# Transposing by DMA instead of on TensorE in a two-layer graph attention kernel

## The reference

```python
def layer0(x, adj):                 # one head, softmax over the query axis
    alpha = relu((x @ wq0) @ (x @ wk0).T) * (adj != 0)
    return softmax(alpha, axis=1) @ (x @ w0)

def layer1(y, adj):                 # 16 heads of 32
    q, k, v = heads(y @ Wq + bq), heads(y @ Wk + bk), heads(y @ Wv + bv)
    s = where(adj == 0, -inf, q @ k.T / sqrt(32))
    return merge(softmax(s, axis=-1) @ v) @ Wo + bo

y   = layernorm(x + layer0(x, adj))
out = layernorm(y + layer1(y, adj))
```

## Time and profile before

| | us |
|---|---|
| median of 3 runs (lowest and highest) | 2967.58 (2967.09 to 2967.93) |
| the profiled execution, span from first to last instruction | 2967.6 |
| one pass, from one group's load to the next | 89.65 |
| TensorE busy in the span | 2902.2 |
| VectorE busy | 2365.3 |
| ScalarE busy | 2016.6 |
| GpSimd busy | 582.6 |
| share of the 16 DMA engines taken by the SP queue's packets | 23.3% |

### The profile page before, as it was taken

How to read it: one execution, slowest core, us unless ns; L and a number is a source line. 1 busy time by engine, 2 the same in 40 slices (tenths; PEclk the granted TensorE clock), 3 DMA queues, 4 the chain that set the end, 5 groups by cost and what they waited for, 6 DMA issues and landing times. The chain is left out here.

```text
span 2967.6 us, 65967 instructions
## 1 busy us (share of the span) xinstructions
PE 2902.2 (98%) x24264; PEld 1775.5 (60%) x24264; DVE 2365.3 (80%) x4627; ACT 2016.6 (68%) x6414; POOL 582.6 (20%) x1289
## 2 busy tenths in 40 slices
PE   7899999999999999999999999999999999999996
PEld 4565666656666656666666666666666666666554
DVE  4588888888888788888788888888888888888886
ACT  3476676666676766676767766767776766776665
POOL 1121122121122121121121221121221211221210
PEclk9999999999999999999999999999999999999997
DMA  3222122222122222122221122221122221222220
GB/s 121 61 72 76 43 56 73 57 76 72 37 65 61 69 76 62 40 72 54 76 76 54 48 72 54 76 76 47 51 76 54 76 76 42 57 71 59 75 53 24
DMA packets 96369, 188.06 MB, mean 63 GB/s; under 512 B 18608, under 2 KB 34992, under 8 KB 96048
## 3 DMA queue, kind: packets, MB, share of 16 engines
q1 hardware_dynamic: 96048, 183.84, 23.3%
HBM read 49.55 MB, written 33.55 MB: 28 GB/s over the span
## 5 line engine op out<-in xcount | busy, mean ns | idle before, releaser
L647 ACT ACTIVATE e<-sm,nmax 128x128 f32<-128x128 f32 x2048 | 791.1, 391 | 27.6 <-DVE nmax L776 25.6
L598 ACT ACTIVATE qk<-front,bqk 128x512 f16<-128x512 f32 x256 | 175.9, 687 | 381.6 <-PE front L429 381.6
L825 POOL TENSOR_TENSOR ln<-ln 128x1 f32<-128x1 f32 x256 | 49.0, 192 | 1890.2 <-DVE ln L804 1496.6
L647 ACT ACTIVATION_READ_ACCUMULATOR e<-sm,nmax 128x1 f32 x2048 | 391.0, 191 | 0.0
L664 DVE SCALAR_TENSOR_TENSOR pT<-pt_bank,pT 128x512 f16<-128x512 f32 x512 | 348.9, 681 | 42.6 <-ACT pT L653 42.1
L653 ACT ACTIVATE pT<-pt_bank 128x512 f16<-128x512 f32 x512 | 302.8, 591 | 103.6 <-PE pt_bank L543 101.6
L776 DVE TENSOR_REDUCE nmax<-sm 128x4 f32<-128x512 f32 x512 | 351.3, 686 | 17.7
L429 PE MATMUL fin_bank<-W_O,oT 128*128 128x512 f16 x1536 | 356.3, 382 | 1.4 <-DVE oT L664 1.4
L429 PE MATMUL front<-W_V,yT 128*128 128x512 f16 x1536 | 354.0, 380 | 0.0
L429 PE MATMUL front<-xT,W_A 128*128 128x512 f16 x1536 | 353.6, 380 | 0.3 <-DVE xT L664 0.3
L429 PE MATMUL front<-yT,W_Q 128*128 128x512 f16 x1536 | 352.2, 379 | 1.6 <-DVE yT L664 1.6
(11 more groups left out here) (111 smaller groups left out, 4482.3 us busy)
## 6 DMA issues: line engine op xcount, KB each, us to landing
q_st<-qk SPq DMA_DIRECT2D x384, 128.0 KB, 2.4
k_st<-qk SPq DMA_DIRECT2D x384, 128.0 KB, 2.4
x_sb<-in_x SPq DMA_DIRECT2D x128, 256.0 KB, 3.4
out_x<-z_sb SPq DMA_DIRECT2D x128, 256.0 KB, 2.5
adj_i<-in_adj SPq DMA_DIRECT2D x32, 256.0 KB, 4.6
y_sb<-in_L_gnn_wq SPq DMA_DIRECT2D x1, 1024.0 KB, 5.6
yb<-in_L_gnn_wk SPq DMA_DIRECT2D x1, 1024.0 KB, 8.1
x_p<-in_L_gnn_weight SPq DMA_DIRECT2D x1, 1024.0 KB, 10.5
```

Of the source, the lines that this page charges most:

```text
L598: i = act.activation(dst, src, ACT.Identity, bias=bias, scale=scale)
L647: act.activation(e1[:, k % 2, h, :], sm[:, k % SM_BUFS, h, :], ACT.Exp, bias=nmax[:, k % SM_BUFS, h:h + 1], accum_out=esum[:, n % 2, head: ...
L825: pool.tensor_tensor(ln[:, 8:9], ln[:, 7:8], ln[:, 8:9], ALU.add).then_inc(moments, 1)
```

## The change

The five kinds of transpose leave TensorE. Their inputs are first split into fp16 HI and LO parts in SBUF, side by side, and one DMA from the SP queue transposes both parts at once. For x: `x_parts` (HI on ScalarE, LO now on VectorE instead of GpSimd), then DMA `xT`. For y: `y_parts` (HI on ScalarE, LO on GpSimd), then DMA `yT`. For the probabilities: `P` (HI and LO from `e1` in SBUF instead of from PSUM), then DMA `pT`, from two buffers `p_p` into four buffers `pT`. For the attention output: `o_parts` (HI on ScalarE, LO on GpSimd), then DMA `oT`. For adj: DMA `adjT` of the fp16 tile `adj01`. Each of these DMAs moves 128 partitions of 1024 fp16 values (256 KB, eight blocks of 128x128), `adjT` 512 values (128 KB, four blocks). The `q` and `k` steps wait for all four `yT` DMAs of the group, `t` for all four `xT` DMAs.

The freed banks go to the front jobs (four banks instead of three) and to `S` (two instead of one). The stacking is cut into eight pieces of three DMAs that other steps can stand between. The order is a new list, `PASS`, with ages from -1 to 2, which also gives the first and the last passes (no order of its own for the drain). Two memsets of eps per normalisation go (the addition is fused on GpSimd), and the scale X_SCALE moves from the evictions to the parts and the normalisation.

The core of the diff:

```diff
-LATE = (2, 3)
-def pass_order(): ...
-def drain_order(): ...
+P_BUFS = 2
+PT_BUFS = 4
+PASS = [
+    ...
+    ("norm1", 2, 2), ("PV", 0, 1), ("norm0", 0, 0), ("y_parts", 0, 0), ("pT", 4, 1), ("oT", 0, 1),
+    ("g", 1, 0), ("S", 5, 1), ("pT", 5, 1), ("yT", 0, 0), ("residual1", 3, 1), ("fin", 3, 2), ("PV", 1, 1), ("o", 0, 1),
+    ("exp", 4, 1), ("P", 4, 1), ("exp", 5, 1), ("o_parts", 0, 1), ("norm0", 1, 0), ("g", 2, 0), ("PV", 2, 1), ("PV", 3, 1),
+    ("P", 5, 1), ("y_parts", 1, 0), ("yT", 1, 0), ("norm0", 2, 0), ("g", 3, 0), ("S", 6, 1), ("y_parts", 2, 0), ("v", 3, 1),
+    ("norm0", 3, 0), ("S", 7, 1), ("yT", 2, 0), ("PV", 4, 1), ("yT", 3, 0), ("y_parts", 3, 0), ("pT", 6, 1), ("exp", 6, 1),
+    ("pT", 7, 1), ("S", 8, 1), ("S", 9, 1), ("P", 6, 1), ("exp", 7, 1), ("S", 10, 1), ("P", 7, 1), ("exp", 8, 1),
+    ("fin", 0, 1), ("S", 11, 1), ("load", 0, -1), ("norm1", 3, 2), ("PV", 5, 1), ("P", 8, 1), ("pT", 8, 1), ("exp", 9, 1),
+    ("pT", 9, 1), ("xT", 0, -1), ("S", 12, 1), ("P", 9, 1), ("q", 0, 0), ("q", 1, 0), ("pT", 10, 1), ("S", 13, 1),
+    ("exp", 10, 1), ("x_parts", 0, -1),
+]
+def schedule(groups):
+    ages = [age for _, _, age in PASS]
+    return [(what, k, p - age) for p in range(min(ages), groups + max(ages)) for what, k, age in PASS if 0 <= p - age < groups]
...
@@ SyncE
+                elif what == "xT":
+                    sp.wait_ge(xlo_ready, count(g, GB, k + 1))
+                    sp.dma_start_transpose(xT[:, k, :, :, :].rearrange("p a t n -> p (a t) n"),
+                                           parts[:, k, :, :].rearrange("p a d -> p (a d)")).then_inc(xT_turned, 16)
+                elif what == "yT":
+                    sp.wait_ge(ylo_ready, count(g, GB, k + 1))
+                    if k == 0 and g:
+                        sp.wait_ge(f_full, yT_read(g - 1))
+                    sp.dma_start_transpose(yT..., parts...).then_inc(yT_turned, 16)
+                elif what == "pT":
+                    sp.wait_ge(plo_ready, count(g, STEPS, k + 1))
+                    wait(sp, pv_done, count(g, STEPS, k + 1 - PT_BUFS))
+                    sp.dma_start_transpose(pT..., p_p...).then_inc(pT_turned[k % PT_BUFS], 16)
+                elif what == "oT":
+                    sp.wait_ge(olo_ready, count(g, GB, k + 1))
+                    wait(sp, fin_full, count(g, GB, k))
+                    sp.dma_start_transpose(oT..., o_p...).then_inc(oT_turned, 16)
...
@@ TensorE
-                if what == "xT":
-                    for n in range(GB):
-                        mm = pe.transpose(bank[:, n * P:(n + 1) * P], x_sb[:, n, k * P:(k + 1) * P], ident[:, :])
-                elif what == "pT":
-                    for h in range(4):
-                        mm = pe.transpose(pt_bank[:, h * P:(h + 1) * P], e1[:, k % 2, h, :], ident[:, :])
                 elif what in ("q", "k"):
                     if k == 0:
-                        pe.wait_ge(f_free, jobs_done(g, "yT", GB - 1))
+                        pe.wait_ge(yT_turned, count(g, 16 * GB, 16 * GB))
...
@@ ScalarE
-                elif what == "pT":
-                    act.wait_ge(pt_full, count(g, STEPS, k + 1))
-                    act.activation(pT[:, k % 2, HI, :], pt_bank[:, :], ACT.Copy, scale=P1_SCALE).then_inc(pthi_ready, 1)
+                elif what == "P":
+                    act.wait_ge(exp_done, count(g, 4 * STEPS, 4 * (k + 1)))
+                    n = count(g, STEPS, k) - P_BUFS
+                    if n >= 0:
+                        act.wait_ge(pT_turned[n % PT_BUFS], 16 * (n // PT_BUFS + 1))
+                    act.activation(p_p[:, k % P_BUFS, HI, :], e1[...], ACT.Copy, scale=P1_SCALE).then_inc(phi_ready, 1)
```

More of the change, by code:

```diff
@@ L112, in order @@
[L112 to L135, removed]
@@ L139 @@
[L139 to L158, removed]
+PASS = [
+    ("xT", 1, 0), ("P", 10, 2), ("exp", 11, 2), ("pT", 11, 2), ("o", 1, 2), ("x_parts", 1, 0), ("P", 11, 2), ("PV", 6, 2),
+    ("o_parts", 1, 2), ("q", 2, 1), ("PV", 7, 2), ("xT", 2, 0), ("x_parts", 2, 0), ("q", 3, 1), ("oT", 1, 2), ("xT", 3, 0),
+    ("S", 14, 2), ("stack_q", 0, 1), ("exp", 12, 2), ("P", 12, 2), ("exp", 13, 2), ("x_parts", 3, 0), ("stack_q", 1, 1),
[18 rows of a table added]
+    ("exp", 10, 1), ("x_parts", 0, -1),
+]
@@ L297, in wait @@
                 eng.wait_ge(s, value)
-        def run_passes(eng, step):
-            for p in (0, 1):
-                for what, k in order(0, p):
-                    step(what, k, (None, p - age(what, k)))
-            for g in range(2, groups):
-                for what, k in order(0, 2):
-                    step(what, k, (None, g - age(what, k)))
-            for what, k, n in drain_order():
-                step(what, k, (None, groups - n))
-        def job_number(at, job, jobs=JOBS):
-            n = jobs.index(job)
-            late = [m for m, j in enumerate(jobs) if age(*j)]
-            if is_at(at, 0):
-                n += sum(m > n for m in late)
-            if is_at(at, groups):
-                n = late.index(n)
-            return count(at, len(jobs), n)
@@ L323, in jobs_done, with run_steps @@
-        def jobs_done(at, *job):
-            return job_number(at, job) + 1
-        def his_done(at, *job):
-            return job_number(at, job, HI_JOBS) + 1
-        def front_bank(at, *job):
-            assert len(JOBS) % len(fbank) == 0
-            place = (None, 0) if is_at(at, 0) else (None, groups) if is_at(at, groups) else (None, 1)
-            return fbank[job_number(place, job) % len(fbank)]
-        def v_pass(g, k):
-            return before(g, -age("v", k))
-        def raw(parts):
-            return parts.bitcast(F32).rearrange("p (t o) -> p t o", t=KT)
+        def run_steps(step):
+            for what, k, g in steps:
+                step(what, k, g)
@@ L367, in _ @@
             sp.dma_start(bo_all[:, :], bo.rearrange("(a d) -> a d", a=1).to_broadcast([P, D])).then_inc(bias_loaded, 16)
-            def load(g):
-                if not is_at(g, 0):
-                    sp.wait_ge(f_free, jobs_done(before(g, 1), "g", GB - 1))
-                for b in range(GB):
-                    src = x_d[g[1] if g[0] is None else g[0]]
-                    sp.dma_start(x_sb[:, b, :], src[b, :, :]).then_inc(x_loaded, 16)
-                wait(sp, adj01_ready, count(g, 1, 0))
-                src = adj_d[g[1] if g[0] is None else g[0]]
-                sp.dma_start(adj_i[:, :, :], src).then_inc(adj_loaded, 16)
@@ L381, in stack @@
-            def stack(n, f):
-                dst, parts = ((q_st, (HI, LO, HI)), (k_st, (HI, HI, LO)))[n]
-                sp.wait_ge(f_free, jobs_done(f, "qk"[n], KT - 1))
-                wait(sp, s_full, count(f, STEPS, 0))
-                for r in range(4):
-                    for row, part in enumerate(parts):
-                        sp.dma_start(dst[row * DH:(row + 1) * DH, r, :, :],
-                                     qk[r * DH:(r + 1) * DH, n, part, :, :]).then_inc(stacked[n], 16)
@@ L391, in store @@
-            def store(b, g):
-                sp.wait_ge(out_ready, count(g, GB, b + 1))
-                dst = out_d[g[1]] if g[0] is None else out_d[g[0] + g[1]]
-                sp.dma_start(dst[b, :, :], z_sb[:, b % 2, :]).then_inc(out_stored[b % 2], 16)
-            steps = [w for w in pass_order() if w[0] in ("norm1", "stack", "load_next")]
-            cut = steps.index(("load_next", 0))
-            def run(these, at, ages=(0, 1, 2)):
-                for what, k in these:
-                    if age(what, k) in ages and what == "stack":
-                        stack(k, at)
-                    elif age(what, k) in ages:
-                        store(k, before(at, age(what, k)))
@@ L421, in _ @@
+            run_steps(step)
             for n in range(2):
@@ L557, in step @@
                     mm.then_inc(pv_done, 1)
[L558 to L563 removed]
                 elif what == "fin":
[L565 removed]
+                    pe.wait_ge(oT_turned, count(g, 16 * GB, 16 * (k + 1)))
```

317 lines of the change are left out of this document (149 added, 168 removed), and 29 rows, old and new, of tables (LATE_ATTENTION, PASS).

## The result

| | before | after |
|---|---|---|
| median of the runs, us | 2967.58 | 2860.97 (2858.67 to 2868.11) |
| after over before, 95% interval | | 0.9643 [0.9629, 0.9657] |
| profiled execution and its span, us | 2967.6 | 2860.47 and 2858.6 |
| one pass, us | 89.65 | 86.0 (29 passes in 2494.13 us, load to load) |

What follows compares the result with a forecast made beforehand. TensorE, busy end to end, was taken as the bound: 2967.6 us less 30 passes x 12.56 us of removed transposes plus 30 x 1.6 us of waits gives 2639 us, likeliest 2640, forecast case 2550 to 2780 (chance 0.48).

Steps and rivals of the forecast that it cites:

- What landing costs: Waits for transposing DMAs to land: 1.4 us per pass at q 0 for y plus 0.2 smaller, 1.6 in all.
- 77.1: TensorE's work in us per pass once 12.56 us of transposes leave its 89.65 us pass.
- 5.3 + L: Time in us from g 3 to y's last landing; L, a DMA's landing time, taken as 2.4 to 4.6.
- For the probabilities this is covered: At P, waiting for the pT landing two steps earlier: two steps have 9.6 us, so landing may average 8 us.
- These two thresholds decide the case: SP queue time per transposing DMA: cover ends at 2.05 us, the whole gain is gone at 2.49 us.
- T: SP queue time of one 256 KB transposing DMA, taken as 1.3 us, giving 55.7 us of queue per pass.
- VectorE comes to about 67 us: VectorE's work per pass after the change, said to cost nothing beside TensorE's 77.1 us.
- Nothing to gain or lose: Splitting the probabilities from SBUF instead of PSUM: VectorE's 681 ns unchanged, as ScalarE took 625 against 611.
- half of it is given back: Rival at the in-order SP queue: waiting steps delay transposes, or T nears 2.05; 2780 to 2960 us, chance 0.12.
- Short gaps might also lower TensorE's clock: Remark within the half-given-back rival: TensorE's clock, 1.00 in the pass, might fall; no size given.
- The two rivals on the price of a transposing DMA: SP queue: 2.6 us per DMA makes it the bound, up to 3600 us (0.18); blocks singly, 3.5 us, beyond 3600 (0.17).

Runs made afterwards that it cites:

- e1: Changed kernel with one list item moved, fin 0 from behind S 10 to behind S 7: 2947.5 us.
- e2: Changed kernel with three buffers p_p for the split probabilities instead of two: 2813.0 us.
- e4: Changed kernel with the 16 pT DMAs per group as plain copies, so the probabilities are not transposed: 2782.1 us.
- e9: Changed kernel with the DMA adjT moved from behind nine of the twelve k copies to ahead of the first: 2821.8 us.
- e13: Changed kernel with both three p_p buffers and adjT ahead of the k copies: 2761.5 us.
- e14: e13 plus plain copies in place of the pT transposes and only 8 of 24 stacking copies from the second group on: 2755.0 us.
- e16: e14 plus GpSimd's LO subtractions of y and the attention output cut to 64 of 512 columns: 2723.4 us.
- e5: Changed kernel with twelve unused matmuls per pass added on TensorE, four each after S 7, S 8 and S 9: 2875.8 us.
- e15: Changed kernel with adjT ahead of the k copies and the 24 stacking DMAs issued from GpSimd's queue: 3115.0 us.

## Why the prediction was wrong

**The step that failed is "What landing costs"**, the term of 1.6 us of waits per pass. Measured, TensorE's waits were 6.3 us per pass, and 2.6 us of lower clock came with them: 8.9 in place of 1.6. The sum with them, 2967.6 - 30 x 12.56 + 30 x 8.9 = 2858, is the profiled execution within 3 us. As the 8.9 are what a measured pass has above 77.1, this shows that 30 passes, and first passes and drain as even, held; that 77.1 held is shown by the slow `fin`, which by itself accounts for 2.5 of the 2.6. So what was removed was right. What would be waited for was not: the term looked for one stall, TensorE at `q` 0 for y. Of the 6.3 us, 4.0 are TensorE at `S` behind VectorE, which the text put at nothing, and so was the clock, named only in a rival.

**Where it was looked for.** The text put the tight place at y. Its chain was longer than taken: the step behind `g` 3 started on TensorE at 1529.05 us and the last `yT` landed at 1542.8, 13.7 us against 5.3 + L. VectorE took `g` 3 only at 1531.76, GpSimd ended `y_parts` 3 at 1538.36 (6.6 us of chain in place of 5.3), and this `yT`, issued at once, landed after 4.4 us. `q` 0 waited for it only 9.4 us in the whole run, though: the `S` gap and the slow `fin` covered it. Loosened by itself (e1) the wait appears, 27 us.

**"For the probabilities this is covered: ... L may reach 8 us on average."** The longest landing of a `pT` was 7.9 us, and the wait was still the largest of ScalarE, 289 us. The allowance was an average over a pass; the list has steps in bursts, two `pT` DMAs stand side by side, and one behind loads landed after 5.4 us. With a third buffer 48 us came back (e2).

**"These two thresholds decide the case."** T was on the right side of 2.05 and 2.49, with a median of 1.26 us, and the queue was busy issuing for some 59 us of a pass by the trace, against 55.7. That T came out was luck in part: it was scaled by size from copies of 128 KB at 0.62 us each, and by that rule a copy of 256 KB should take 1.25; in e4 it took 0.48. But a queue in order holds by sequence as well as by sum: `adjT` stood behind 21 stacking copies (39 us, e9). The text counted each moved DMA's cost and not what it stands behind. The two holds together, this one and the two buffers, are 99.5 us (e13), nearly all that the queue and its landings cost, as e14 adds 6.5.

**"VectorE comes to about 67 us ... All lie beside TensorE's 77.1 and cost nothing while that is so."** VectorE's sum was near (69.2 us in one pass), but over eight us it had 7.4 us of work while TensorE had 3.7, and the three waits come in every pass. And the split out of SBUF does not cost 681 ns: its mean is 766. "Nothing to gain or lose" rested on ScalarE's two rows, carried over to VectorE. With GpSimd's subtractions short, 31.6 us came back (e16). What is left then, 2723 against 2639, is 2.8 us of `S` wait and 2.0 of lower clock per pass (79.15 us busy in a pass of 81.92 against 77.1), less the 1.6 taken: 30 x 3.2 = 96, about the 84 that are missing. So of the 222 us between forecast and result some 106 are the queue and its landings, 32 the splits beside GpSimd, and 84 the `S` gap with its clock. The first two were removed by runs; the last is a sum of records. No run removed the gap alone: e5 raised the clock and lost time, with 53 us of new waits at `PV` and 2.6 us of its own matmuls per pass (an estimate, twelve at 216 ns).

**The rivals.** The case that came is "half of it is given back", in part by the mechanism it named: transposes that leave late in the in-order queue (about half of what is missing), and the clock ("Short gaps might also lower TensorE's clock"). It did not name VectorE, behind which 4.0 of the 6.3 us were waited; that its example also has 6.3 us of waits is chance. It had 0.12. The forecast had 0.48 because the queue's sum left 21 us free; that was an argument on averages. The two rivals on the price of a transposing DMA were wrong by their own number, 1.26 us against 2.6 and 3.5. The condition of the first was met, as the packets were many and small, and shows in the engines' time (1.4 us against 0.6) and not in the queue's. Of what had been said to show them, DMAs over 2 us are 63 of 928 in after and 185 in e15, and TensorE waited for `pT` at `PV` for only 9 us in the whole run of each; in e15 it waited for `xT`.

The price question is thus settled by the rows, at medians of 1.24 to 1.29 us to issue and 2.5 to 3.2 to land. Of the two figures of the Trainium skill weighed there, 261 GB/s ("DMA: Bandwidth & Descriptors", Latency and other measured facts), an estimate of 1.0 us, was near (1.26 us of the queue, about 1.4 of the engines), and 1309 ns per block ("VectorE: DVE Perf Modes", The three transpose paths) is not a price that eight blocks of one DMA pay one after another.

## What to carry to other kernels

When work moves from a full engine to an in-order DMA queue, check the queue by what each transfer stands behind and by how many buffers its producer has, and not by its sum; here both together were worth 99.5 us, nearly as much as the whole gain of 107. Look at each stretch of a few microseconds for the next engine that is full there: an average of 77% hid 7.4 of 8 us. When a local fix at the visible gap loses time, ask which engine is late there before moving more work to the other. Test edits again once a hold is gone: the same one was worth 9 us with the queue's holds and 32 without.

## What the runs showed of the hardware

**VectorE and GpSimd block each other.** VectorE's split reads two SBUF operands and takes 0.68 us alone. Beside GpSimd's subtraction it took 1.42, in after, where GpSimd came first:

```profile
1530.13 1.16 POOL L705 TENSOR_TENSOR o_p<-o_sb,o_p 128x512 f16<-128x512 f32 x1
```

```profile
1530.42 1.42 DVE L546 SCALAR_TENSOR_TENSOR p_p<-e,p_p 128x512 f16<-128x512 f32 x1
```

GpSimd ended at 1531.29 and VectorE at 1531.84, 0.55 us later: it looks like a whole wait, not a slower pace. The same holds at 1514.21 (1.37 us, 0.54 after GpSimd's end). Steps that read PSUM beside SBUF (`sm`, `bT`, `v_p`) stayed at 680 to 682 ns. In the other direction GpSimd's addition `yb` took 1.72 us at 1514.99, where one by itself took 1.27, and 1.50 in the mean. The Trainium skill, page "SBUF — State Buffer" (SBUF: two separate sides), says that the two engines share one pair of ports as an exclusive lock when VectorE has two SBUF inputs and GpSimd reads SBUF. The trace agrees, and the prediction had not drawn on it.

**The clock falls behind a short gap.** After a stretch of 8 us with TensorE busy 3.67, the granted clock was 0.58 in the next 7 us, in after, and a step of 12 matmuls of 512 columns took 5.12 us from start to start instead of 2.59. In the kernel before it was 1.00 from 300 to 2800 us. With matmuls put into the gap (e5) the mean clock of the run rose from 0.953 to 0.971.

**Transposing DMAs take engine time.** About 1.4 us for 256 KB against 0.6 for a plain copy of the same tile, both estimated from the shares in after, before and e4. Their issue takes a median of 1.26 us of the queue against 0.48 for the copy. In e15, with another queue's copies in flight, single ones took 4.15 and 5.55 us.
